# Row maxima interleaved with scores in the attention phases of a two-layer kernel

## The chip, the core and the metric

The kernel runs on one core of a Trainium2 chip. The metric is the device time of one execution in microseconds. Every kernel is timed several times and the median is given; the profile is of one execution more, with its own time.

## What is computed

Two layers on x of 2 x 1024 rows of 128: attention with 16 heads of 64, an expert layer with one expert chosen for each row, a state-space layer, and a dense layer over 8 experts. Only attention is touched:

```python
Q = jnp.einsum('btd,hkd->bthk', x, W_Q) + b_Q
K = jnp.einsum('btd,hkd->bthk', x, W_K) + b_K
V = jnp.einsum('btd,hkd->bthk', x, W_V) + b_V
scores = jnp.einsum('bqhk,bshk->bhqs', Q, K) / jnp.sqrt(jnp.asarray(d_head, x.dtype))
attn = jax.nn.softmax(scores, axis=-1)
out_h = jnp.einsum('bhqs,bshk->bqhk', attn, V)
return jnp.einsum('bqhk,hdk->bqd', out_h, W_O) + b_O
```

## The kernel before

Heads go in pairs, so the two batches have 16 pairs (0 to 15). The two heads of a pair stand on the two halves of the array: for scores and row maxima on the two row halves (64*128 in the profile), for projection, value products, values and sums on the two column halves (128*64). The rows of a sequence are cut into two chunks c of 512 columns, its keys into eight tiles j of 128.

A pair has four phases f. In phase f the kernel makes four scores ("score", for chunk f // 2 and four of the key tiles), and four value products ("pv") of the same tiles. A score (pe_score, L563 and L567) is a matmul of high and low parts, three products and one that subtracts the row's maximum (guard), each on both row halves, eight matmuls in all. ScalarE takes its exponential (L1065) into one of seven prob buffers; the value product (pe_pv, L594) reads that buffer, and GpSimd adds it to the sums (L2013).

The maxima that are subtracted are those of a later pair's rows, and are made while this pair is worked on: "max" (pe_max, L580) is one matmul on each row half with the high parts alone, "maxed" is the reduction by VectorE (dve_max, L1494). When all 16 of a pair are there, "cols" (L1504), "row" and "rowed" turn them into a row, which a DMA spreads into guard. Phase 3 makes maxima for the pair after the next. "proj" (L610) is the projection of a coming pair's keys or queries, followed by a high part by ScalarE (L1039) and a low part by VectorE ("lo", L1487). "values" (L625) and "valued" (L1523, VectorE) make the values of the next pair in phase 1. "out" (L672) is the output product of the pair before, which VectorE adds into x in eight instructions (L1555), in phases 2 and 3; "sum" (L645) makes the divisors from the sums, in phase 0. "take" is ScalarE's copy of the finished value products (L1074). Some phases also have steps of the next stages, from the table EARLY.

One list of steps, built by phase() for pairs 0 to 14 and by last_phase() for pair 15, sets the order on every engine: each engine walks through the list and issues the steps that are its own, in that order. So the order of "score" and "max" in the list is the order in TensorE's queue, and that of "maxed", "lo", "valued" and "out" the one in VectorE's.

PSUM has three slots of two banks for scores, maxima and output products, one bank for the value products that are being summed, and one work bank for projection, values, row and sum. The slots are given in turn, in the order of the list (Banks.plan): each score, maximum or output product waits until the reader of the one three places earlier is done (slots.free): the exponential of a score, the reduction of a maximum, VectorE's group of an output product.

Of the kernel before, what the change touches and what calls it, by code (L numbers as in the profile page):

```python
# [183 lines left out]
def project(pair, chunk):  # L184
    return [("proj", pair, *chunk), ("lo", pair, *chunk)]


def largest(*maxes):

    return [step for m in maxes for step in (("max", *m), ("maxed", *m))]  # L190


def phase(pair, f):


    if pair == LAST:
        return last_phase(f)
    c, js = f // 2, range(NT // 2 * (f % 2), NT // 2 * (f % 2 + 1))
    last, nxt = pair - 1, pair + 1
    if pair == 0:  # L200
        maxes = [(nxt, *m) for m in MAXES[max(6 * f - 2, 0):6 * f + 4]] if f < 3 else [(nxt + 1, *m) for m in MAXES[:4]]
    else:
        maxes = [(nxt, *MAXES[4 * f + 4 + i]) if f < 3 else (nxt + 1, *MAXES[i]) for i in range(4)]
    maxes = [m for m in maxes if m[0] < PAIRS]
    ahead = pair + 2 if f < 3 else pair + 3
    chunks = [(ahead, CHUNKS[(f + 1) % 4])] if ahead < PAIRS else []
    projected = project(*chunks[0]) if chunks else []
    products, found = [("max", *m) for m in maxes], [("maxed", *m) for m in maxes]
    pv = [("pv", pair, c, j) for j in js]
    early = EARLY.get((pair, f), [])  # L210
    order = [("score", pair, c, j) for j in js] + largest(*maxes[:1]) + projected[:1] + pv[:1]
    order += products[1:4] + projected[1:] + found[1:3]
    if f == 1:
        order += [pv[1], ("values", nxt, 0), ("valued", nxt, 0)] + found[3:4]
    else:
        order += found[3:4] + [pv[1]]
    order += largest(*maxes[4:])
    if f == 2:
        order.append(("cols", nxt))
    if f >= 2 and last >= 0:  # L220
        order.append(("out", last, f - 2))
    order.append(pv[2])
    if f == 0:
        order += [("sum", last)] * (last >= 0) + [pv[3]] + early
    elif f == 1:
        order += [pv[3], ("values", nxt, 1), ("valued", nxt, 1)] + early + [("take", pair, c)]
    elif f == 2:
        order += early + [pv[3], ("row", nxt), ("rowed", nxt)]
    else:
        order += early + [pv[3], ("take", pair, c)]  # L230
    return order


def last_phase(f):

    pair, c, js = LAST, f // 2, range(NT // 2 * (f % 2), NT // 2 * (f % 2 + 1))
    order = [("score", pair, c, j) for j in js]
    if f == 1:
        order += [("out", pair - 1, 0), ("out", pair - 1, 1)]
    second = ([("sumhalf", pair, 0)] if f == 3 else []) + EARLY.get((pair, f), [])  # L240
    pv = [("pv", pair, c, j) for j in js]
    order += pv[:2] + second + pv[2:3] + [("sum", pair - 1)] * (f == 0) + pv[3:]
    if f % 2:
        order.append(("take", pair, c))
    if f == 3:
        order.append(("out", pair, 0))
    return order
# [6 lines left out]
def attention_order():  # L254

    order = [("gsum",), ("lnvar", 0), ("lnroot", 0), ("gscale",), ("lnrows", 0), *turned(0), ("bias", 0)]
    keys, queries, more_keys, more_queries = (("proj", 0, *ch) for ch in CHUNKS)
    maxes = [(0, *m) for m in MAXES]
    order += [keys, queries, *largest(*maxes[:2]), more_keys, more_queries, *largest(*maxes[2:4])]
    order += [("full", 0, *ch) for ch in CHUNKS] + largest(maxes[4]) + ahead_of_scores(1, CHUNKS[0]) + largest(*maxes[5:7])  # L260
    order += ahead_of_scores(1, CHUNKS[1]) + largest(*maxes[7:9]) + [("values", 0, 0)] + largest(*maxes[9:11])
    order += ahead_of_scores(1, CHUNKS[2]) + largest(*maxes[11:13]) + ahead_of_scores(1, CHUNKS[3]) + largest(maxes[13])
    order += [("values", 0, 1)] + largest(maxes[14]) + ahead_of_scores(2, CHUNKS[0]) + largest(maxes[15])
    order += [("gdir",), ("cols", 0), ("row", 0), ("valued", 0, 0), ("rowed", 0), ("valued", 0, 1)]
    for pair in range(PAIRS):
        for f in range(4):
            order += phase(pair, f)
    return order
# [2253 lines left out]
```

## Time and profile before

| what | value |
|---|---|
| median of 3 runs | 1196.02 us (1195.93 to 1198.23) |
| span of the profiled execution | 1192.9 us |
| TensorE busy | 1129.3 us, 95% |
| VectorE busy | 816.6 us, 68% |
| GpSimd busy | 759.8 us, 64% |
| ScalarE busy | 600.7 us, 50% |

Attention takes the first 740 us or so of the span. Busy time of an engine is the time in which at least one of its instructions runs; matmuls are pipelined, so the time from the start of one to the start of the next says more than the length shown. In the timeline, instructions of one kind that follow each other are merged into one line with their count; what stands in brackets is the idle time before it and who ended that. PE is TensorE's matmuls, PEld its weight loads, DVE VectorE, ACT ScalarE, POOL GpSimd.

### The profile page before, as it was taken

How to read it: one execution, taken by the hardware profiler on the slowest of the kernel's cores; microseconds unless marked ns; L12 is line 12 of the kernel's file. 1: busy time of each engine (PE TensorE's matmuls, PEld its weight loads, DVE VectorE, ACT ScalarE, POOL GpSimd, SP SyncE). 2: the span in 40 equal slices, each digit the busy share in tenths (PEclk: the TensorE clock that was granted, in tenths of full speed). 3: DMA queues.
4: the chain of work that ended last, by engine and by line, in shares of the span. 5: the costliest groups of instructions: out<-in, count | busy, mean ns of one | idle time of the engine just before them, and what ended most of it. 6: DMA issues, size and time to landing. Idle time of an engine off the chain costs nothing.

```text
span 1192.9 us, 19525 instructions
## 1 busy us (share of the span) xinstructions
PE 1129.3 (95%) x7549; PEld 660.4 (55%) x7549; DVE 816.6 (68%) x1208; ACT 600.7 (50%) x867; POOL 759.8 (64%) x393
## 2 busy tenths in 40 slices
PE   5899999999999999999999999988888998989998
PEld 1445555555555555555555555776644444445786
DVE  5575666655755656655666754723798999998887
ACT  3434345344343444444444344544886664956753
POOL 3477778777777768767678973023089887896100
PEclk9899999999999999999999999998999999999999
DMA  6000000000000000000000204357464544341000
GB/s 199 1 1 2 1 1 1 2 1 1 2 1 2 1 2 1 2 2 1 1 1 11 68 30 147 111 148 223 147 219 135 167 142 158 127 159 54 10 9 18
DMA packets 38076, 68.85 MB, mean 58 GB/s; under 512 B 5952, under 2 KB 24128, under 8 KB 37984
## 3 DMA queue, kind: packets, MB, share of 16 engines
q1 hardware_dynamic: 34976, 64.52, 17.1%
q0 software_dynamic: 1024, 2.10, 0.5%
q8 instruction: 60, 0.98, 0.3%
q10 hardware_dynamic: 1984, 0.98, 0.3%
q14 instruction: 32, 0.26, 0.1%
HBM read 61.30 MB, written 6.16 MB: 57 GB/s over the span
## 4 chain that ended last, share of the span: by engine, by line
PE 78%; issue 7%; DVE 6%; POOL 5%; ACT 2%; DMA 2%; SPq 0%; POOLq 0%; DVEq 0%; ACTq 0%
PE psum L594 20%; PE psum L563 16%; PE psum L580 6%; PE psum L610 6%; PE psum L567 5%; PE psum L974 3%; PE psum L672 3%; PE psum L880 3%; PE psum L957 3%; POOL hc L2101 3%; PE psum L625 2%; PE psum L645 2%; PE psum L749 2%; PE psum L738 1%; DVE psum L1781 1%
## 5 line engine op out<-in xcount | busy, mean ns | idle before, releaser
L2013 POOL TENSOR_TENSOR psums<-psums,prob 128x1024 f32<-128x1024 f32 x180 | 426.9, 2372 | 106.4 <-ACT prob L1065 84.3
L1494 DVE TENSOR_REDUCE mx<-psum 128x2 f32<-128x1024 f32 x256 | 301.8, 1218 | 214.2 <-PE psum L580 214.2
L1065 ACT ACTIVATE prob<-psum 128x1024 f32<-128x1024 f32 x256 | 243.4, 1025 | 218.2 <-PE psum L567 218.2
L594 PE MATMUL psum<-prob,V 128*64 128x512 f32 x1024 | 258.4, 604 | 0.0
L2101 POOL TENSOR_TENSOR hc<-hs,cc 128x1024 f32<-128x1024 f32 x64 | 151.5, 2368 | 21.5 <-DVE hs L1788 19.0
L1788 DVE TENSOR_TENSOR_SCAN hs<-dA,psum 128x1024 f32<-128x1024 f32 x64 | 146.3, 2287 | 2.2
L880 PE MATMUL psum<-hc,ident 128*128 128x512 f32 x256 | 123.6, 606 | 2.5 <-DVE slot_rows_h L1796 1.4
L594 PEld LDWEIGHTS psum<-prob,V 128*64 128x64 f32 x1024 | 62.0, 136 | 98.3 <-issue 92.6
L2013 POOL TENSOR_TENSOR psums<-prob 128x1024 f32<-128x1024 f32 x30 | 71.4, 2382 | 63.4 <-ACT prob L1065 63.4
L563 PE MATMUL psum<-q_hi,k_hi 64*128 64x512 f32 x512 | 108.4, 419 | 0.0
L567 PE MATMUL psum<-guard,row_one 64*128 64x512 f32 x512 | 101.6, 393 | 2.2 <-DMA guard<-mrow 2.2
L563 PE MATMUL psum<-q_hi,k_lo 64*128 64x512 f32 x512 | 101.7, 393 | 0.0
L563 PE MATMUL psum<-q_lo,k_hi 64*128 64x512 f32 x512 | 101.6, 393 | 0.0
L580 PE MATMUL psum<-k_hi,q_hi 64*128 64x512 f32 x512 | 90.2, 425 | 4.0 <-DVE mx L1494 2.3
L1074 ACT COPY oraw<-psum 128x512 f32<-128x512 f32 x32 | 18.8, 587 | 131.8 <-PE psum L594 131.8
L580 PEld LDWEIGHTS psum<-k_hi,q_hi 64*128 64x128 f32 x512 | 43.8, 186 | 67.5 <-issue 48.9
L1555 DVE SCALAR_TENSOR_TENSOR x<-psum,inv,x 128x128 f32<-128x128 f32 x256 | 71.9, 343 | 12.1 <-issue 10.7
L880 PEld LDWEIGHTS psum<-hc,ident 128*128 128x128 f32 x256 | 48.8, 194 | 44.7 <-issue 32.4
L563 PEld LDWEIGHTS psum<-q_hi,k_hi 64*128 64x128 f32 x512 | 48.5, 186 | 38.2 <-issue 17.3
L864 PE MATMUL psum<-xdr,pickr 128*128 128x512 f32 x128 | 57.7, 533 | 10.8 <-DVE hs L1788 10.6
L1287 ACT ACTIVATE dA<-slotT,alog 128x1024 f32<-128x1024 f32 x32 | 36.6, 1150 | 40.0 <-DVE hs L1788 39.7
L567 PEld LDWEIGHTS psum<-guard,row_one 64*128 64x128 f32 x512 | 48.8, 186 | 13.7 <-DMA guard<-mrow 2.6
(290 smaller groups left out, 1686.9 us busy)
## 6 DMA issues: line engine op xcount, KB each, us to landing
cc<-C_rows SPq DMA_DIRECT2D x64, 512.0 KB, 3.7
kq_wts<-in_e_rows SPq DMA_DIRECT2D x14, 578.0 KB, 4.7
e_wts<-in_e_rows SPq DMA_DIRECT2D x10, 578.0 KB, 4.1
e_w<-in_e_rows SPq DMA_DIRECT2D x6, 578.0 KB, 4.3
slots_in<-e_zero SPq DMA_DIRECT2D x2, 960.0 KB, 8.2
slots_out<-e_y SPq DMA_DIRECT2D x30, 64.0 KB, 3.0
x<-in_x SPq DMA_DIRECT2D x2, 512.0 KB, 5.0
e_w<-in_e_w SPq DMA_DIRECT2D x1, 1024.0 KB, 7.8
```

The lines of the kernel that those rows point to most:

```text
L563: pe.matmul(both[:, s, :], left[HALF[s], js], right[HALF[s], cs], start=(part == 0), stop=False)
L567: ins = pe.matmul(both[:, s, :], A.row_one[HALF[s], :], A.guard[q][HALF[s], cs], start=False, stop=True)
L580: ins = pe.matmul(both[:, s, :], A.q_hi[r][HALF[s], t * P:(t + 1) * P], A.k_hi[r][HALF[s], c * CH:(c + 1) * CH], start=True, stop=True)
L594: ins = pe.matmul(A.O[HALF[s], :], A.V[pair % 2][:, j, s * DH:(s + 1) * DH], A.prob[unit(pair, c, j) % NPB][:, s * CH:(s + 1) * CH], start ...
L610: ins = pe.matmul(bank[HALF[s], :], w[:, (2 * p + s) * DH:(2 * p + s + 1) * DH], K.xnT[:, b, c * CH:(c + 1) * CH], start=True, stop=True)
L880: ins = pe.matmul(X.Y[:, c * CH:(c + 1) * CH], K.ident[:, :], X.hc[u % 3][:, c * CH:(c + 1) * CH], start=(u > 0 and n == 0), stop=(n == NS ...
L1065: act.activation(A.prob[n % NPB][:, :], slots.bank("score", pair, c, j).rearrange("p s n -> p (s n)"), ACT.Exp, scale=float(DH) ** -0.5).t ...
L1494: dve.tensor_reduce(K.A.mx[:, :, t, c], slots.bank("max", pair, t, c), AXX, ALU.max).then_inc(*slots.inc("max", pair, t, c))
L1555: ins = dve.scalar_tensor_tensor(out=K.x[:, tile, :], in0=slots.bank("out", pair, c)[:, s, t * P:(t + 1) * P], scalar=A.inv[:, s * NT + 4 ...
L1788: dve.tensor_tensor_scan(X.hs[u % 3][:, :], X.dA[u % 3][:, :], X.gain[u % 2], 0.0, ALU.mult, ALU.add).then_inc(X.state_done, 1)
L2013: pool.tensor_tensor(total[:, :], (K.A.prob[(n - 1) % NPB] if j == 1 else total)[:, :], K.A.prob[n % NPB][:, :], ALU.add).then_inc(*K.psum ...
L2101: pool.tensor_tensor(X.hc[u % 3][:, :], X.hs[u % 3][:, :], X.cc[u % NCC][:, :], ALU.mult).then_inc(X.product_done, 1)
```

## The change

The change is in phase() alone. Before, a phase's list was: four scores, the first maximum with its reduction, the projection, the first value product, three maxima, the low part of the projection and the reductions, the second value product. Now each of the first four maxima, with its reduction, stands ahead of one of the four scores; then come the projection with its low part and the first two value products. In phase 1 the first half of the values follows these, without the reduction that stood behind it. Further maxima (pair 0 has up to six in a phase), cols, out and all after these stay where they are.

```diff
@@ -208,12 +208,13 @@
     products, found = [("max", *m) for m in maxes], [("maxed", *m) for m in maxes]
     pv = [("pv", pair, c, j) for j in js]
     early = EARLY.get((pair, f), [])
-    order = [("score", pair, c, j) for j in js] + largest(*maxes[:1]) + projected[:1] + pv[:1]
-    order += products[1:4] + projected[1:] + found[1:3]
+    scores = [("score", pair, c, j) for j in js]
+    order = []
+    for i, score in enumerate(scores):
+        order += largest(*maxes[i:i + 1]) + [score]
+    order += projected + pv[:2]
     if f == 1:
-        order += [pv[1], ("values", nxt, 0), ("valued", nxt, 0)] + found[3:4]
-    else:
-        order += found[3:4] + [pv[1]]
+        order += [("values", nxt, 0), ("valued", nxt, 0)]
     order += largest(*maxes[4:])
     if f == 2:
         order.append(("cols", nxt))
```

largest() gives for each maximum the steps "max" and "maxed".

## Rows read from the trace of the kernel before

**Rows 1.** The page: busy time and share of the span of each engine.

```profile
PE 1129.3 (95%) x7549; PEld 660.4 (55%) x7549; DVE 816.6 (68%) x1208; ACT 600.7 (50%) x867; POOL 759.8 (64%) x393
```

**Rows 2.** Busy time by stretch: start:end, length, then each engine, TensorE's clock last.

```profile
44.00:49.50 5.50, 5.50 (x26) 4.32 (x28) 0.00 (x0) 3.07 (x3) 1.94 (x1) 0.50 0.00 0
...
200.00:740.00 540.00, 539.26 (x4439) 303.61 (x4436) 327.86 (x518) 233.22 (x279) 398.25 (x176) 1.00 0.04 13
```

**Rows 3.** Timeline of TensorE over phase 1 of a pair: start, length, engine, line.

```profile
509.96 0.50 PE L563 MATMUL psum<-q_hi,k_hi 64*128 64x512 f32 x2
...
513.54 0.39 PE L567 MATMUL psum<-guard,row_one 64*128 64x512 f32 x2
513.77 0.40 PE L580 MATMUL psum<-k_hi,q_hi 64*128 64x512 f32 x2
514.09 1.08 PE L610 MATMUL psum<-xnT,wk 128*64 128x512 f32 x4
515.00 1.03 PE L594 MATMUL psum<-prob,V 128*64 128x512 f32 x4
...
516.85 1.08 PE L594 MATMUL psum<-prob,V 128*64 128x512 f32 x4
...
518.64 1.89 PE L594 MATMUL psum<-prob,V 128*64 128x512 f32 x8
520.35 1.04 PE L625 MATMUL psum<-wv,xnT 128*64 128x128 f32 x16
521.33 0.50 PE L563 MATMUL psum<-q_hi,k_hi 64*128 64x512 f32 x2
```

**Rows 4.** The same phase, timeline of the other engines.

```profile
511.20 3.80 ACT L1065 ACTIVATE prob<-psum 128x1024 f32<-128x1024 f32 x4 [6.78 <-PE psum L567]
...
514.21 1.23 DVE L1494 TENSOR_REDUCE mx<-psum 128x2 f32<-128x1024 f32 x1 [4.79 <-PE psum L580]
515.22 0.69 ACT L1039 ACTIVATE k_hi<-psum,bk 128x512 fp32r<-128x512 f32 x1 [0.23 <-PE psum L610]
...
515.94 0.75 DVE L1487 SCALAR_TENSOR_TENSOR k_lo<-psum,bk,k_hi 128x512 fp32r<-128x512 f32 x1 [0.51 <-ACT k_hi L1039]
...
516.61 2.35 DVE L1494 TENSOR_REDUCE mx<-psum 128x2 f32<-128x1024 f32 x2
...
521.44 0.69 DVE L1523 TENSOR_TENSOR V<-psum,bv 128x512 f32<-128x512 f32 x1 [0.76 <-PE psum L625]
```

**Rows 5.** Timeline before the first phase: maxima that wait for VectorE.

```profile
30.34 2.35 DVE L1494 TENSOR_REDUCE mx<-psum 128x2 f32<-128x1024 f32 x2
...
31.61 0.19 PEld L580 LDWEIGHTS psum<-k_hi,q_hi 64*128 64x128 f32 x2 [0.53 <-DVE mx L1494]
...
32.04 0.65 PE L610 MATMUL psum<-xnT,wk 128*64 128x512 f32 x2
...
36.85 0.50 PE L580 MATMUL psum<-k_hi,q_hi 64*128 64x512 f32 x2
...
37.40 1.23 DVE L1494 TENSOR_REDUCE mx<-psum 128x2 f32<-128x1024 f32 x1 [0.19 <-PE psum L580]
```

**Rows 6.** Timeline at the starts of two phases with VectorE work of the later stage.

```profile
191.87 0.50 PE L563 MATMUL psum<-q_hi,k_hi 64*128 64x512 f32 x2
192.86 0.64 DVE L1449 BATCH_NORM_AGGREGATE mv<-stats 128x2 f32<-128x6 f32 x8
...
618.01 0.50 PE L563 MATMUL psum<-q_hi,k_hi 64*128 64x512 f32 x2
619.94 0.17 DVE L1642 CAST e_owneri<-e_owner 128x15 int32<-128x15 f32 x1
```

**Rows 7.** Timeline: an output product and the VectorE group that reads it.

```profile
739.66 1.95 PE L672 MATMUL psum<-wo,oraw 64*128 64x128 f32 x32
740.82 4.49 DVE L1555 SCALAR_TENSOR_TENSOR x<-psum,inv,x 128x128 f32<-128x128 f32 x16 [4.42 <-issue]
```

**Rows 8.** Timeline before the first phase: the longest wait of TensorE there.

```profile
43.91 0.80 PE L567 MATMUL psum<-guard,row_one 64*128 64x512 f32 x2 [2.20 <-DMA guard<-mrow]
```

## The prediction

> **What bounds the kernel now.** I read the page first. TensorE is busy for 95% of the span, VectorE for 68%, no other engine for more [rows 1]. The busy time by stretch says it more sharply: from 200 to 740 us TensorE is busy for 539.26 of 540.00 us at clock 1.00, VectorE for 327.86, ScalarE for 233.22 and GpSimd for 398.25 [rows 2]. So in attention the order of TensorE's own queue is the time, and every other engine follows it. That leaves two ways to change the time: TensorE's work gets shorter or longer by itself, or a wait appears in a queue that now has none. The change does both, so I took one phase apart.
>
> **What a phase costs.** Phase 1 of a pair runs from 509.96 to 521.33 [rows 3]. A score is four pairs of matmuls on the two row halves of the array; pairs follow each other by 0.23 us (513.54 to 513.77), so a score takes 0.93 and a row maximum 0.23. Value products work on the two column halves, 0.86 each (518.64 to 520.35 is two of them). Projection to value product is 0.91. The first pair of rows after column work takes 0.10 more. Start to the projection: 514.09 - 509.96 = 4.13, which is 0.10 + 4 x 0.93 + 0.23 and 0.09 for the change to columns. From the first value product to the second are 516.85 - 515.00 = 1.85, though the product takes 0.86 and the three maxima 0.69: going to rows and back to columns costs 0.30.
>
> **Part one: a round trip goes.** Today a phase goes to rows twice before its value products are under way (scores and first maximum, then three maxima); after the change once. The trip's 0.30 is saved in every phase that has maxima: 59 (pairs 0 to 14 have 60 phases, and the last of them has no maxima left; pair 15 has an order of its own, untouched). Saved: 59 x 0.30 = 17.7 us. The out products on rows in phases 2 and 3 keep their own trip.
>
> The Trainium skill, page "TensorEngine Tiling (Array Packing)", section "Key Properties", says that changing the tiling mode drains TensorE. The trace agrees, with the 0.30 above; by this rule alone the change would be a gain of 17.7 us.
>
> **Part two: a wait comes.** Scores and maxima share three PSUM slots in turn, so each instruction waits for the reader of the slot three places earlier. Today S0 S1 S2 S3 M0 come in a row, and the readers of S0 and S1 (exponentials) have two scores' time; M0's reader (the VectorE reduction) has the projection, a value product and two maxima. After the change the queue is M0 S0 M1 S1 M2 S2 M3 S3, and S1 takes M0's slot. Between them lie S0 and M1 only.
>
> How long is a maximum's slot held? The reduction starts 0.44 after its matmuls (513.77 to 514.21), 0.55 where these pay the change to rows (36.85 to 37.40), and takes 1.22 to 1.23 [rows 3 to 5]. The release is seen where maxima already wait for VectorE, ahead of the first phase: the reduction begun at 30.34 ends at 31.56, and TensorE starts at 31.61, 0.05 later; it then needs 0.43 to the next work (32.04) where an unhindered maximum needs 0.32 (513.77 to 514.09), because its weights were not loaded beside earlier work: 0.10 more [rows 3, 5].
>
> Now the run, with time 0 at M0. S0 at 0.33, M1 at 1.26, and S1 could start at 1.49. M0's slot is released at 0.55 + 1.22 + 0.05 = 1.82, and S1 counts as started at 1.92: 0.43 late. M2 is then at 2.85. M1's reduction starts when VectorE is free, at 1.70, its slot is loaded for S2 at 3.07, and S2 could start at 3.08: no wait. M2's reduction starts at 3.29, so S3 counts as started at 3.29 + 1.22 + 0.05 + 0.10 = 4.66 and ends at 5.59. M3 waits for S1's exponential: an exponential starts 1.24 after its score's first pair when the load is not hidden (509.96 to 511.20) and takes 1.01 (four with three steps of 0.93 between them take 3.80) [rows 4], so M3 is at about 4.2, which is still ahead of S3's limit. Without any wait the run would end at 0.10 + 4 x 1.16 = 4.74. The waits cost 0.85 a phase, and the change to columns comes as before.
>
> Before, these parts took 4.13 + (1.85 - 0.86) = 5.12; after 5.59 + 0.09 = 5.68. Net +0.56 (0.85 of waits less the 0.30 of part one). 59 x 0.56 = 33.0 us. Queued behind each wait on TensorE is everything, as it runs in order: the next maximum, the projection and all value products.
>
> **Part three: what VectorE does when a phase starts.** Today the first reduction comes 4.3 us into the phase, and whatever VectorE still has from the phase before is covered (its idle time ahead of 514.21 is 4.79) [rows 4]. After the change M0's reduction is due at 0.55, and each microsecond that VectorE is busy beyond that moves S1 and all behind it.
> Values: after phase 1 the second value addition runs from 521.44 to 522.13, phase 2 having begun at 521.33. With the next instruction issued some 0.07 before its end the reduction starts at 0.74, 0.19 late, in 15 phases: 2.9 us [rows 3, 4].
> Output groups: VectorE starts 1.16 after an out product and takes 4.49/2 = 2.25 for one; the next phase starts about 2.9 after the product (half of 1.95 and a trip of 0.2, and two value products). It ends at 0.5: nothing [rows 7].
> Later stages' steps: the statistics end 1.63 after their phase began (191.87, 193.50), which costs 1.1, twice; the owner list ends 2.10 after (618.01, 620.11), of which the value addition has 0.19: 1.4; four smaller ones of the same kind I put at 1.6 together, an estimate from these two. 5.2 us [rows 6].
> Projection: it keeps the single work bank until VectorE has written the low part. Now the high part waits for the fourth exponential (at about 6.8) and takes 0.69, the low part 0.75: 8.3. The first values product in phase 1 is due at 5.68 + 0.91 + 2 x 0.86 = 8.3 and needs the bank and its weights at 8.4: 0.14 in 14 phases, 2.0 us. In the other phases the bank's next user comes later: nothing.
> GpSimd adds the probabilities and is busy for 398 of 540 us [rows 2]; the phase gets longer, its work does not: nothing. The row and its DMA stay where they were behind the value products, a whole phase or more ahead of their reader: nothing. DMA queues are not moved past.
>
> **Sum.** 33.0 + 2.9 + 5.2 + 2.0 = 43.1 us. The profiled execution has a span of 1192.9, the median is 1196.0, so 3.1 lie outside; 1196.0 + 43 = 1239.
>
> Bounds: each wait has its nearest row, but no row shows a score that waits for a reduction. At the low end the weights' load is hidden after a wait and the maximum counts 0.44: S1 and S3 are 0.10 each, S1 another 0.11 earlier, 0.31 a phase or 18 us less, and part three's later stages come to nothing: 1239 - 18 - 5 = 1216. At the high end M3's wait adds to S3's and every reduction is late by what its issue costs behind another (1.23 instead of 1.13 apart), 0.25 a phase: 1254. I take the middle, as 0.10 and 0.55 are rows of the same matmul.
>
> **Rivals.**
> (a) Faster: slots come back in time and only the trip is gone, 1196.0 - 17.7 = 1178. It decides at 1.39 us from a maximum to the score two places on; the rows give 0.44 + 1.22 + 0.05 = 1.71. For it speaks that the two scores in a row of today never wait, and that a wait's attribution in a trace is inferred. Against it, the waits that maxima have ahead of phase 0.
> (b) Small waits: only S1 waits, or S3's wait falls under M3's, so that waits are 0.43 to 0.5 a phase: net 0.13 to 0.2, which is 8 to 12 us, and with 2 to 10 of part three 1206 to 1218; at the point where waits are 0.30, no change, 1196.
> (c) VectorE as the bound: all three of S1, S2 and S3 wait as long as S1 (3 x 0.43), and leftovers of VectorE push on from phase to phase by 0.1: 1.4 a phase instead of 0.85, 59 x 0.55 = 32 more, 1271. Against: VectorE works 327.86 of 540 us.
> (d) The clock falls. After the wait of 2.20 us that ends at 43.91, TensorE ran from 44.0 to 49.5 at clock 0.50 (1.2 GHz), and a stretch like this costs half its 5.5 us [rows 2, 8]. The new waits are 0.3 us each, and short waits of 0.2 to 0.5 before phase 0 left the clock high. Were there one such stretch in each of 15 pairs, 41 us more: 1280.
> The Trainium skill, page "TensorE: Matmul & The Clock Gate", section "A second HAM failure mode: psum-queue depth-cycling", describes a kernel whose small idle gaps between groups, from cycling through PSUM banks, make the clock oscillate; that is (d).
>
> **How the numbers follow.** Forecast 0.68; (a) 0.11; (b) 0.15, of which 0.03 within 0.2%; (c) 0.04; (d) 0.02. The forecast's own range is 1216 to 1254; taking in (b) but for its no-change end, the range is 1206 to 1254, and (a), (c), (d) and that end, 0.20 together, are left out. A measurement of this kernel can tell about 0.2% from no change. Faster 0.11, same 0.03, slower 0.68 + 0.12 + 0.04 + 0.02 = 0.86.
>
> **What would show it.** In the profile after: TensorE's busy share in attention falls below 95%, with idle time ahead of L563's weight loads released by the reduction L1494, about 0.3 to 0.4 ahead of S1 and 0.1 to 0.2 ahead of S3, none ahead of S2; phases of 11.9 to 12.1 us where they were 11.4; four reductions close together from 0.55 after a phase's start; the projection directly followed by two value products at 0.86 each; clock 1.00. The prediction is wrong if a score can start without the reduction's release, if the reduction starts much sooner than 0.44 after its matmuls, or if the change to rows costs more than 0.30 elsewhere.

## The result and the profile after

The changed kernel takes 1231.24 us (median of 4 runs, 1229.62 to 1232.13), the kernel before 1195.97 beside it; the ratio is 1.0286 with a 95% interval of [1.0274, 1.0298]. It is 35 us slower, where the prediction had 43 (1239, range 1206 to 1254).

The page after: the same number of instructions, TensorE at 93%, and a first row of slices that still looks full. The stretch from 200 to 740 us, which answers to [rows 2], shows a loss: 526.71 us busy where it was 539.26, with the clock at 1.00 as before. It shows only about half of it: a matmul is drawn 0.40 us long where the next follows 0.23 behind it, so the first 0.17 of a wait lies under the matmul before. (In the changed kernel all lines below the edit have a number one higher: L564 is a score, L581 a maximum, L595 a value product, L1495 the reduction.)

```profile
span 1229.6 us, 19525 instructions
...
PE 1146.0 (93%) x7549; PEld 653.3 (53%) x7549; DVE 829.3 (67%) x1208; ACT 617.6 (50%) x867; POOL 759.9 (62%) x393
...
PE   5899999999999999999999999996979999889998
...
PEclk9899999999999999999999999998999999999999
```

```profile
200.00:740.00 540.00, 526.71 (x4187) 282.44 (x4185) 325.33 (x494) 236.11 (x269) 385.02 (x171) 1.00 0.02 7
```

The waits from 60 to 780 us (engine, line, waited for: us in total, times, longest):

```profile
PEld psum L564 <- DVE mx L1495: 61.5, 147, 2.1
...
PEld psum L581 <- ACT prob L1066: 22.4, 57, 0.4
...
PE psum L564 <- DVE mx L1495: 17.1, 57, 1.7
```

In the trace before, the reduction L1494 held TensorE up in attention almost nowhere. Now 147 weight loads of scores (L564) wait for it, 61.5 us in all and 2.1 us at most, and 57 of maxima (L581) wait for exponentials. These sums are idle time of the weight loads, much of it beside matmuls that still run; what a wait costs is read from the starts of the steps below. M0 to M3 are the maxima of a phase, S0 to S3 its scores.

This is phase 1 of the pair whose phase stands in [rows 3] and [rows 4]: start, length, engine, line.

```profile
530.73 0.50 PE L581 MATMUL psum<-k_hi,q_hi 64*128 64x512 f32 x2
...
531.06 0.39 PE L564 MATMUL psum<-q_hi,k_hi 64*128 64x512 f32 x2
...
531.27 2.39 DVE L1495 TENSOR_REDUCE mx<-psum 128x2 f32<-128x1024 f32 x2 [1.08 <-PE psum L581]
...
532.55 0.19 PEld L564 LDWEIGHTS psum<-q_hi,k_hi 64*128 64x128 f32 x2 [0.60 <-DVE mx L1495]
532.55 0.51 PE L564 MATMUL psum<-q_hi,k_hi 64*128 64x512 f32 x2 [0.16 <-DVE mx L1495]
...
533.59 0.40 PE L581 MATMUL psum<-k_hi,q_hi 64*128 64x512 f32 x2
...
533.83 0.39 PE L564 MATMUL psum<-q_hi,k_hi 64*128 64x512 f32 x2
...
534.87 0.19 PEld L581 LDWEIGHTS psum<-k_hi,q_hi 64*128 64x128 f32 x2 [0.39 <-ACT prob L1066]
...
535.32 0.18 PEld L564 LDWEIGHTS psum<-q_hi,k_hi 64*128 64x128 f32 x2 [0.26 <-DVE mx L1495]
...
536.44 1.08 PE L611 MATMUL psum<-xnT,wk 128*64 128x512 f32 x4
...
537.35 1.89 PE L595 MATMUL psum<-prob,V 128*64 128x512 f32 x8
...
539.10 1.09 PE L626 MATMUL psum<-wv,xnT 128*64 128x128 f32 x16
...
542.71 0.50 PE L581 MATMUL psum<-k_hi,q_hi 64*128 64x512 f32 x2
```

Times from the phase's start at 530.73, beside the run that the prediction worked out: S1 loads at 1.82 (1.82), S2 starts at 3.10 (3.08, no real wait), M3 at 4.14 (4.2), S3 at 4.59 (4.56), the projection at 5.71 (5.68). The bracket of S1's weight load names the reduction. After the projection two value products and the values follow in one run, 1.75 us from the first product to the values: 0.86 each and 0.03.

The whole of attention, by the starts of its phases in the two traces (us, mean of the pairs without work of a later stage):

| phase | before | after | more | predicted |
|---|---|---|---|---|
| 0 | 11.50 | 12.00 | 0.50 | 0.56 |
| 1 | 11.37 | 11.96 | 0.59 | 0.70 |
| 2 | 11.23 | 11.80 | 0.57 | 0.75 |
| 3 | 10.98 | 11.37 | 0.39 | 0.56 |

From the first phase's start to the last pair's are 685.1 us before and 718.9 after, 33.8 more. The rest of the program has 3.1 more in this pair of profiles, but it ranged from 465.3 to 472.3 us over all twelve profiles of this study, whose kernels are alike there; that part is not the change's.

### The profile page after: what moved, and what is told of

Its sections match the earlier page's. It is cut to its first block, busy times and chain, and to the rows that moved or that the text cites. A ratio compares the mean times of both kernels' runs of the same rounds, so it can differ in the third digit from the quotient of the medians.

```text
span 1229.6 us, 19525 instructions
## 1 busy us (share of the span) xinstructions
PE 1146.0 (93%) x7549; PEld 653.3 (53%) x7549; DVE 829.3 (67%) x1208; ACT 617.6 (50%) x867; POOL 759.9 (62%) x393
## 4 chain that ended last, share of the span: by engine, by line
PE 67%; DVE 17%; issue 8%; POOL 4%; ACT 2%; DMA 1%; another core or an unknown queue 0%; SPq 0%; POOLq 0%; ACTq 0%; DVEq 0%
PE psum L595 15%; PE psum L564 14%; DVE mx L1495 6%; PE psum L611 5%; PE psum L581 4%; PE psum L568 4%; DVE x L1556 4%; PE psum L975 3%; PE psum L881 3%; PE psum L958 3%; POOL hc L2102 2%; PE psum L626 2%; PE psum L646 2%; PE psum L673 2%; PE psum L750 1%
## 5 line engine op out<-in xcount | busy, mean ns | idle before, releaser
L1066 ACT ACTIVATE prob<-psum 128x1024 f32<-128x1024 f32 x256 | 261.1, 1026 | 283.8 <-PE psum L568 275.5
L1495 DVE TENSOR_REDUCE mx<-psum 128x2 f32<-128x1024 f32 x256 | 307.8, 1224 | 60.9 <-PE psum L581 59.5
L595 PE MATMUL psum<-prob,V 128*64 128x512 f32 x1024 | 245.4, 598 | 0.0
L564 PE MATMUL psum<-q_hi,k_hi 64*128 64x512 f32 x512 | 114.4, 443 | 17.3 <-DVE mx L1495 17.3
L595 PEld LDWEIGHTS psum<-prob,V 128*64 128x64 f32 x1024 | 67.3, 137 | 110.9 <-issue 90.0
L581 PE MATMUL psum<-k_hi,q_hi 64*128 64x512 f32 x512 | 115.8, 451 | 3.3 <-DVE mx L1495 1.6
L564 PE MATMUL psum<-q_lo,k_hi 64*128 64x512 f32 x512 | 101.3, 392 | 0.0
L564 PE MATMUL psum<-q_hi,k_lo 64*128 64x512 f32 x512 | 101.3, 392 | 0.0
L564 PEld LDWEIGHTS psum<-q_hi,k_hi 64*128 64x128 f32 x512 | 48.3, 185 | 70.3 <-DVE mx L1495 62.5
L581 PEld LDWEIGHTS psum<-k_hi,q_hi 64*128 64x128 f32 x512 | 48.3, 186 | 67.5 <-issue 28.4
```

Of the source, the lines that this page charges most:

```text
L564: pe.matmul(both[:, s, :], left[HALF[s], js], right[HALF[s], cs], start=(part == 0), stop=False)
L581: ins = pe.matmul(both[:, s, :], A.q_hi[r][HALF[s], t * P:(t + 1) * P], A.k_hi[r][HALF[s], c * CH:(c + 1) * CH], start=True, stop=True)
L595: ins = pe.matmul(A.O[HALF[s], :], A.V[pair % 2][:, j, s * DH:(s + 1) * DH], A.prob[unit(pair, c, j) % NPB][:, s * CH:(s + 1) * CH], start ...
L1066: act.activation(A.prob[n % NPB][:, :], slots.bank("score", pair, c, j).rearrange("p s n -> p (s n)"), ACT.Exp, scale=float(DH) ** -0.5).t ...
L1495: dve.tensor_reduce(K.A.mx[:, :, t, c], slots.bank("max", pair, t, c), AXX, ALU.max).then_inc(*slots.inc("max", pair, t, c))
```

## The experiments

The theory: (T) a phase now contains two slot times of a maximum in series (M0's ahead of S1, M2's ahead of S3), 0.85 us, and saves one trip to rows. Rivals to it, in capitals to tell them from those of the prediction: (A) maxima and scores in turn are dear on TensorE by themselves; (B) VectorE's load is the bound. Each ratio is to runs of the kernel before on the same chip.

### A shorter reader, in the changed kernel and in the kernel before

```diff
-    dve.tensor_reduce(K.A.mx[:, :, t, c], slots.bank("max", pair, t, c), AXX, ALU.max).then_inc(*slots.inc("max", pair, t, c))
+    dve.tensor_reduce(K.A.mx[:, :, t, c], slots.bank("max", pair, t, c)[:, :, 0:CH // 2], AXX, ALU.max).then_inc(*slots.inc("max", pair, t, c))
```

> The changed kernel, but each reduction of a maximum reads only the first 256 of the 512 columns of each head: it leaves out half of the keys in the row maxima. Theory (a score waits for the slot of the maximum three places earlier, and the gain is the saved trip to rows): a reduction falls from 1.22 us to about 0.7, so M0's slot is back at about 1.3 us where S1 could start at 1.49; no score waits for a reduction. Maxima then wait for exponentials (M2 for S0, 0.2 us a phase). A phase is shorter than the kernel before's by 0.15 in phases 0 to 2 and up to 0.3 in phase 3: about 1184 us (1180 to 1190), that is 47 below the changed kernel. Rival A (alternating maxima and scores is dear by itself, on TensorE): stays within 10 us of 1231. Rival B (VectorE's load is the bound): it falls too, but so should the same edit of the kernel before.

> The kernel before with the same shorter reduction (half of the keys left out of the row maxima), the control of the run above. Theory: nothing on TensorE waits for reductions there but the output product in phases 2 and 3, which seems to wait 0.16 us for the second maximum's reduction (1.12 us from value product to output product, where the changed kernel has 0.96): 28 x 0.16 = 4.5 us less, about 1191 (1189 to 1194). Rival B (VectorE's load): it falls by tens of us as well.

Measured: the changed kernel with it 0.9932 [0.991, 0.9955], the kernel before with it 0.9945 [0.9928, 0.9961]. Times 1195.97 that is 1188 and 1189. The same edit takes 42 us (1.0286 less 0.9932) from the changed kernel and 7 from the kernel before. VectorE's load from 200 to 740 us fell alike in both (325.33 to 247.23 us, and 327.86 to 240.49), and only the changed kernel gained tens of us, so the load by itself, (B), is not the bound; the order on TensorE is unchanged, so (A) is out. Phase 1 of the same pair, timeline:

```profile
502.27 0.69 DVE L1495 TENSOR_REDUCE mx<-psum 128x2 f32<-128x512 f32 x1 [1.08 <-PE psum L581]
...
502.99 0.41 PE L581 MATMUL psum<-k_hi,q_hi 64*128 64x512 f32 x2
...
503.23 0.41 PE L564 MATMUL psum<-q_hi,k_hi 64*128 64x512 f32 x2
...
504.28 0.18 PEld L581 LDWEIGHTS psum<-k_hi,q_hi 64*128 64x128 f32 x2 [0.38 <-ACT prob L1066]
...
506.81 0.20 PEld L611 LDWEIGHTS psum<-xnT,wk 128*64 128x64 f32 x4 [0.37 <-issue]
```

The reduction takes 0.69, S1's first pair starts at 503.23, 1.50 after the phase began, with no wait. What is left are two waits of maxima for exponentials, 0.25 together (the run ends at 5.08, unhindered it would be 4.83), which is why a phase gains 0.05 to 0.25 and not 0.35. The expected 1184, in whose range of 1180 to 1190 the result lies, left out that five phases with work of a later stage still lose 0.5 to 1.2 each, 4 us in sum. In the control, phases 2 and 3 are shorter by 0.11: that is the wait of the output product. Phase 2 of pair 0 is shorter by 2.2 in both; its row stands behind six reductions.

### The order within the run

```diff
     for i, score in enumerate(scores):
-        order += largest(*maxes[i:i + 1]) + [score]
+        order += largest(*maxes[:1]) * (i == 0) + [score] + largest(*maxes[i:i + 1]) * (i > 0)
```

> The changed kernel with the run M0 S0 S1 M1 S2 M2 S3 M3: one trip to rows as in the change, but M0 and M1 have two scores behind them. Theory: S1 no longer waits; S2 waits 0.2 for S0's exponential, S3 0.2 for M1's reduction; the run ends at 5.16 us instead of 5.59: 59 x 0.43 = 25 us less than the changed kernel, about 1206 (1200 to 1212), still above the kernel before. Rival A (mixing them in one run costs by itself): near 1231.

Measured: 1.0052 [1.0035, 1.0068], 1202 us: 28 us less than the changed kernel by the ratios, with all reads whole and still one trip.

```profile
512.45 0.50 PE L581 MATMUL psum<-k_hi,q_hi 64*128 64x512 f32 x2
...
513.73 0.40 PE L564 MATMUL psum<-q_hi,k_hi 64*128 64x512 f32 x2
...
515.01 0.19 PEld L564 LDWEIGHTS psum<-q_hi,k_hi 64*128 64x128 f32 x2 [0.40 <-ACT prob L1066]
...
516.36 0.19 PEld L564 LDWEIGHTS psum<-q_hi,k_hi 64*128 64x128 f32 x2 [0.24 <-DVE mx L1495]
...
517.75 1.08 PE L611 MATMUL psum<-xnT,wk 128*64 128x512 f32 x4
```

Against the kernel before it is still 6 us slower. S1 (513.73) waits for nothing; the waits are those expected, S2 for an exponential and S3 for a reduction, and the run ends at 5.30 with the change to columns (expected 5.25). In plain phases it is 0.1 to 0.2 slower than before in phases 0 and 1, and even in 2 and 3. (A) is out a second time: the same instructions in one run, 28 us apart by the order of the slots alone.

### A longer reader

```diff
+    dve.tensor_reduce(K.A.extra[:, :, t, c], slots.bank("max", pair, t, c)[:, :, 0:P // 2], AXX, ALU.max)
     dve.tensor_reduce(K.A.mx[:, :, t, c], slots.bank("max", pair, t, c), AXX, ALU.max).then_inc(*slots.inc("max", pair, t, c))
...
+            A.extra = sba("extra", [P, 2, NT, NC])
```

> The changed kernel with one small reduction (64 columns of each head, into a tile of its own) ahead of each reduction of a maximum: it adds work and takes nothing away. It holds each maximum's slot about 0.2 us longer. Theory: the run's length contains two slot times of a maximum in series (M0's ahead of S1, M2's ahead of S3), so a phase grows by 2 x 0.2 = 0.4 us and the kernel by 59 x 0.4 = 24 us: 1255 (1247 to 1265). Rival B (VectorE's rate of four reductions a phase): 4 x 0.2 x 59 = 47 us more, 1278. Rival A: no change from 1231.

Measured: 1.0507 [1.0477, 1.0538], 1257 us, 26 above the changed kernel by the ratios.

```profile
549.53 0.19 PEld L581 LDWEIGHTS psum<-k_hi,q_hi 64*128 64x128 f32 x2 [0.81 <-issue]
...
550.07 0.29 DVE L1495 TENSOR_REDUCE extra<-psum 128x2 f32<-128x128 f32 x1 [1.08 <-PE psum L581]
...
550.28 1.22 DVE L1496 TENSOR_REDUCE mx<-psum 128x2 f32<-128x1024 f32 x1
...
551.55 0.19 PEld L564 LDWEIGHTS psum<-q_hi,k_hi 64*128 64x128 f32 x2 [0.79 <-DVE mx L1496]
...
552.88 0.19 PEld L564 LDWEIGHTS psum<-q_hi,k_hi 64*128 64x128 f32 x2 [0.34 <-DVE mx L1496]
...
554.49 0.19 PEld L564 LDWEIGHTS psum<-q_hi,k_hi 64*128 64x128 f32 x2 [0.45 <-DVE mx L1496]
...
555.63 1.08 PE L611 MATMUL psum<-xnT,wk 128*64 128x512 f32 x4
```

The small reduction puts the large one back by 0.21 (550.07 to 550.28). S1 loads 2.02 after the start instead of 1.82, the projection comes at 6.10 instead of 5.71: two slot times, not four. The phase grew by 0.4. That is (T)'s number and half of (B)'s.

### One maximum ahead of the scores

```diff
-    order = [("score", pair, c, j) for j in js] + largest(*maxes[:1]) + projected[:1] + pv[:1]
+    order = largest(*maxes[:1]) + [("score", pair, c, j) for j in js] + projected[:1] + pv[:1]
```

> The kernel before with one step moved: the first maximum and its reduction stand ahead of the four scores, the other three maxima stay behind the first value product, so the two trips to rows stay. Theory (what costs in the change is the slot order, not that a maximum stands ahead of a score): M0 has two scores behind it before its slot is needed, no wait in a plain phase; where VectorE still has work of a later stage at the phase's start (five phases) S2 waits up to 1 us: 0 to 4 us more than the kernel before, ratio 1.000 to 1.003. Rival A (a maximum at the head of a phase is dear by itself): more than 10 us.

Measured: 1.0154 [1.0128, 1.0181], 18 us more: the expectation was wrong, and the number alone would speak for (A), which had more than 10. The phases decide. Plain phases 1 and 2 are unchanged to 0.02, so a maximum at the head is not dear by itself; plain phases 3 and the phases 0 after them lose 0.6 and 0.45, and phases with work of a later stage up to 1.5. The timeline across the start of a phase 3, at 356.37:

```profile
355.41 2.29 DVE L1555 SCALAR_TENSOR_TENSOR x<-psum,inv,x 128x128 f32<-128x128 f32 x8
...
356.37 0.50 PE L580 MATMUL psum<-k_hi,q_hi 64*128 64x512 f32 x2
...
357.75 0.19 PEld L563 LDWEIGHTS psum<-q_hi,k_hi 64*128 64x128 f32 x2 [0.40 <-DVE x L1555]
...
357.81 1.22 DVE L1494 TENSOR_REDUCE mx<-psum 128x2 f32<-128x1024 f32 x1
...
359.07 0.19 PEld L563 LDWEIGHTS psum<-q_hi,k_hi 64*128 64x128 f32 x2 [0.57 <-DVE mx L1494]
```

In this kernel the three late reductions still stand ahead of the output product's eight VectorE instructions, which therefore begin at 355.41, one microsecond ahead of the next phase, and not 1.16 after the product. S1 now takes the output product's slot and waits for them (0.40), and M0's reduction starts only at 357.81, so S2 waits as well (0.57). The prediction had costed this leftover at nothing for the changed kernel, rightly, because there the reductions are all done by then. A maximum ahead of the scores pays when VectorE is clear, and not otherwise.

### Output products inside the run of scores

If slots and trips are the price, the output products of phases 2 and 3, which have a trip of their own, should pay when they stand where every slot has its reader's time.

Phase 3 alone:

```diff
-    order = [("score", pair, c, j) for j in js] + largest(*maxes[:1]) + projected[:1] + pv[:1]
+    scores = [("score", pair, c, j) for j in js]
+    within = f == 3 and last >= 0
+    if within:
+        order = largest(*maxes[:1]) + scores[:3] + [("out", last, 1)] + scores[3:] + projected[:1] + pv[:1]
+    else:
+        order = scores + largest(*maxes[:1]) + projected[:1] + pv[:1]
...
-    if f >= 2 and last >= 0:
+    if f == 2 and last >= 0:
```

> The kernel before with phase 3 of pairs 1 to 14 as M0 S0 S1 S2 out S3, projection, P0, three maxima, P1, P2, P3: the output product, which has a trip to rows of its own today, goes into the run of scores, at a place where each slot has its reader's time. Theory: a trip of 0.35 and a wait of 0.11 less in 14 phases, 5 to 6 us less than the kernel before, ratio 0.9955. Rival (VectorE's group of 2.3 us behind the output product holds back the reductions and with them TensorE): no gain or a loss.

Measured: 1.0006 [0.9995, 1.0017], nothing where 5 to 6 us less were expected; this is the rival's outcome. The plain phases 3 are 0.15 to 0.2 longer, for the reason just seen: phase 2's output product keeps VectorE busy across the border, S1 and S2 wait. In pairs 3, 9 and 10, whose phase 2 is longer and lets VectorE finish, phase 3 is 0.41 to 0.50 shorter, and in pair 14, which has no maxima left, 0.39; in pairs 12 and 13 it is 1.08 and 0.61 longer.

Phase 2 alone:

```diff
+    if f == 2 and last >= 0 and projected:
+        order = largest(*maxes[:1]) + scores[:1] + products[1:2] + projected[:1] + products[2:3] + scores[1:2] + found[1:3]
+        order += scores[2:3] + [("out", last, 0)] + scores[3:] + products[3:4] + pv[:1] + found[3:4] + [("cols", nxt)]
+        return order + pv[1:3] + projected[1:] + early + [pv[3], ("row", nxt), ("rowed", nxt)]
```

> The kernel before with phase 2 of pairs 1 to 13 as M0 S0 M1, projection, M2 S1 S2 out S3 M3, then the four value products: two trips to rows instead of three, each slot with its reader's time between. Theory: 13 x 0.4 = 5 us less than the kernel before, ratio 0.9955. Rival as in the run above: no gain or a loss, the row at the phase's end waiting for the late reduction of M3.

Measured: 0.9978 [0.9964, 0.9991], 2.6 us less where 5 were expected. Plain phases 2 take 10.78 instead of 11.23. (Here L585 is a maximum, L615 the projection, L677 the output product, L599 a value product.)

```profile
515.63 0.50 PE L585 MATMUL psum<-k_hi,q_hi 64*128 64x512 f32 x2
...
517.22 1.08 PE L615 MATMUL psum<-xnT,wq 128*64 128x512 f32 x4
...
518.23 0.50 PE L585 MATMUL psum<-k_hi,q_hi 64*128 64x512 f32 x2
...
520.41 1.05 PE L677 MATMUL psum<-wo,oraw 64*128 64x128 f32 x16
...
522.23 0.40 PE L585 MATMUL psum<-k_hi,q_hi 64*128 64x512 f32 x2
...
522.55 0.20 PEld L599 LDWEIGHTS psum<-prob,V 128*64 128x64 f32 x4 [0.37 <-issue]
```

From 518.23 to 522.55 the run M2 S1 S2 out S3 M3 has no wait. The gain of 0.46 in plain phases is a trip of 0.35 and the output product's wait of 0.11. The phases 2 of pairs 3, 9, 10 and 12, and phase 3 of pair 13, lost 0.25 to 0.65 instead; they have steps of the next stage.

Both, with the order of the second experiment in phases 0 and 2 of pair 0:

```diff
+    if pair == 0 and f in (0, 2):
+        order = largest(*maxes[:1]) + scores[:2] + largest(*maxes[1:2]) + scores[2:3] + largest(*maxes[2:3]) + scores[3:]
+        order += largest(*maxes[3:4]) + projected + pv[:2] + largest(*maxes[4:]) + [("cols", nxt)] * (f == 2) + pv[2:3]
+        return order + (pv[3:] + early if f == 0 else early + [pv[3], ("row", nxt), ("rowed", nxt)])
```

> Both moves of the output product together, and phases 0 and 2 of pair 0 in the order M0 S0 S1 M1 S2 M2 S3 M3 with one trip (these two phases were shorter by 0.7 and 1.4 us with that order). Theory: 5.6 + 5.2 + 2.1 = 13 us less than the kernel before, ratio 0.989 (0.987 to 0.993); a version below both kernels.

Measured: 0.9948 [0.9927, 0.9968], 6 us less instead of 13. Now that phase 2 leaves VectorE clear, plain phases 3 have 10.49 to 10.53 instead of 10.99, as expected of them. The rest went in crowded phases: +0.69 and +1.23 in phases 2 and 3 of pair 12, +0.82 in phase 3 of pair 13, 0.3 each in phase 2 of pairs 3, 9 and 10. Pair 0's two phases gave 0.6 and 1.0 of the 2.1 expected of them.

Without the moves there:

```diff
-    if f == 2 and last >= 0 and projected:
+    if f == 2 and last >= 0 and projected and pair not in (3, 9, 12):
...
-    within = f == 3 and last >= 0
+    within = f == 3 and last >= 0 and pair not in (12, 13)
...
-    if f == 2 and last >= 0:
+    if f >= 2 and last >= 0 and not within:
```

> The version with both moves of the output product, without them in the phases where they lost time: phase 2 of pairs 3, 9 and 12 (+0.30, +0.28, +0.69 us) and phase 3 of pairs 12 and 13 (+1.23, +0.82), where steps of the next stage crowd VectorE. Theory (phases add up, and a phase's loss comes from its own readers): 3.3 us less than that version, 11 us less than the kernel before, ratio 0.991 (0.989 to 0.994). Rival (the moves shift waits from phase to phase, so taking some back loses the neighbours' gain): 0.995.

Measured: 0.9913 [0.9897, 0.9929], 1185.6 us by the ratio, 10 below the kernel before and 45 below the changed one, and faster than both; 11 below the kernel before were expected. Pair 12's phases and phase 2 of pairs 3 and 9 are back to their old length; phase 2 of pair 10, which kept the move, still has its 0.25. Phase 3 of pair 13 is not back (+0.68). It lost as much (+0.65) in the kernel with phase 2 alone moved, so that loss comes from the move in the phase ahead of it: the rival has this one case.

### The trip by itself

```diff
-    order += products[1:4] + projected[1:] + found[1:3]
-    if f == 1:
-        order += [pv[1], ("values", nxt, 0), ("valued", nxt, 0)] + found[3:4]
+    if f < 2:
+        order += products[1:3] + projected[1:] + found[1:3] + pv[1:2] + products[3:4]
+        order += [("values", nxt, 0), ("valued", nxt, 0)] * (f == 1) + found[3:4]
+    else:
+        order += products[1:4] + projected[1:] + found[1:3]
+    if f < 2:
+        pass
     else:
         order += found[3:4] + [pv[1]]
```

> The kernel before with one more trip to rows and no other change of what waits: in phases 0 and 1 of pairs 0 to 14 the third of the three maxima stands behind the second value product. It measures the trip by itself, 30 times. By the phases compared so far a trip costs 0.35 us (0.10 into rows, 0.20 out of them for the first weight load and 0.05 on the next product): 10.5 us more, ratio 1.0088. By the prediction's 0.30: 9 us, 1.0075. Rival (the 0.35 are waits of maxima for exponentials, not the change of tiling): less than 3 us, as the third maximum then has more time.

Measured: 1.0104 [1.0083, 1.0125], 12 us for 30 trips. By phases: 26 of the 30 are longer by 0.31 to 0.38, with a mean of 0.35, while phases 2 and 3 are unchanged to 0.03. (Here L584 is a maximum, L598 a value product, L629 the values.)

```profile
522.93 0.73 PE L584 MATMUL psum<-k_hi,q_hi 64*128 64x512 f32 x4
...
523.59 0.20 PEld L598 LDWEIGHTS psum<-prob,V 128*64 128x64 f32 x4 [0.36 <-issue]
...
524.60 0.19 PEld L584 LDWEIGHTS psum<-k_hi,q_hi 64*128 64x128 f32 x2 [0.81 <-issue]
...
525.03 1.09 PE L629 MATMUL psum<-wv,xnT 128*64 128x128 f32 x16
```

From 523.59 to 525.03 are 1.44 us for a value product (0.86) and a maximum (0.23): 0.35 for going back to rows and leaving them once more. No engine is named as waited for in these lines. Of the other four phases two are of pair 0, and two of pair 3 are 1.15 longer; in those the clock fell, as the last section has it.

## Why the prediction was right, point by point

- What bounds the kernel: right. TensorE's queue was full and every change in it moved the time one to one; phases add up, and the extra time of the 60 phases (33.8 us) is the median's 35.3 within what the rest of the program varies.
- Part two, the run with its waits, was right to 0.03 us at each step but M3, which waits 0.06 less than said and costs nothing. It came from rows of the kernel before alone: 0.44 or 0.55 until the reduction starts, 1.22 for it, 0.05 for the release, 0.10 for a weight load that is not hidden. The longer reader confirmed that two slot times are in series; the shorter reader and the other order took the cost away.
- Part one, the trip, was mis-sized: 0.30 predicted, 0.35 measured by itself. The part missed is 0.05 on the first value product after rows (517.76 - 516.85 = 0.91 in [rows 3], against 0.86), 59 x 0.05 = 3.0 us.
- "A wait in a queue that now has none" was not quite so: in phases 2 and 3 the output product already waited for a reduction, 0.11 by the control with the shorter reader. The change does away with it, 28 x 0.11 = 3.1 us. The trace before gave no releaser for it; it showed only as idle time of 0.89 ahead of the output product's weight load, as in the line below, where other changes to rows have 0.81.

```profile
529.31 1.00 PEld L672 LDWEIGHTS psum<-wo,oraw 64*128 64x128 f32 x16 [0.89 <-issue]
```

- Part three, VectorE's leftovers: the value addition cost phase 2 what was said (S1 at 2.00 instead of 1.82). The later stages' steps were put at 5.2; the phases concerned (1 of pairs 3 and 9, 1 to 3 of pair 12, 0 of pair 13) have 5.3 above their like. Output groups: nothing, right. The low part's wait was put at 0.14 a phase and was 0.03: 1.5 us.
- Pair 0 was taken as any other, 2.6 us more, and is 0.4 shorter: its first maximum now fills time in which scores wait for the first guard (2.20 us before, 1.96 after), and in phase 2 its row no longer waits so long for late reductions. 3.0 us. The size is not firm. Both kernels had the clock at 0.50 for 6.8 us in pair 0's phase 0; the kernel with phase 2 alone moved, whose phase 0 there has the order of the kernel before, had 3.4 us of it in its profile, and that phase was 1.3 us shorter.
- These four, 3.0 + 3.1 + 1.5 + 3.0 = 10.6, make the difference of 9.3 between 43.1 and 33.8, but for 1.3.
- Of the signs that were to show it, one failed: TensorE's busy share from 200 to 740 us is 97.5%, not below 95%. A phase is 0.4 to 0.6 longer, but the 0.17 of each wait that lies under the matmul before it does not show as idle time.
- The rivals: (a) fell with the first trace, as S1 waits. (b) fell with the same trace: the projection came at 5.71, so that the waits are 0.88 a phase and not 0.43 to 0.5. Waits of the size that (b) had, some 0.45, came with the order M0 S0 S1 M1 S2 M2 S3 M3, which was measured at 1202. (c) fell there too, as S2 starts with no wait to speak of, and with the longer reader, which added two slot times and not four. (d): the clock was 1.00 from 200 to 740 us in the changed kernel; its waits, some 0.4 us and one of 1.7, did not bring it down. The Trainium skill's account of a clock that oscillates with small gaps ("TensorE: Matmul & The Clock Gate", section "A second HAM failure mode: psum-queue depth-cycling") is not what this kernel shows from 200 to 740 us. With a longer reader the clock fell once, as the last section has it.

## What to carry to other kernels

With slots given in turn, write down for each user the time from its first matmul to its reader's release, and place behind it at least that much of other work before the slot comes round; here the first maximum has 1.49 us until S1 could start, where 1.82 are needed, and needs two scores behind it. A trip between row and column tiling costs 0.35 us, less than the waits that its removal brought; where both can be had (an output product among scores, 0.46 a phase), look first at what the reader's engine still has to do when the phase starts. A step of another stage that today lies under scores has its cover only as long as nobody waits for that engine at once.

## What the runs showed of the hardware that was not expected

The releaser column had no name for waits that end while an engine changes tiling: the idle time reads as "issue" with 0.81 us, and a wait of 0.1 on top of it shows only as 0.89. Comparing the start-to-start times of the same pair of steps in two orders (1.12 and 0.96 from value product to output product: 0.05 of it is the first value product after rows, the rest the wait) found it.

TensorE's clock fell in the middle of attention in two of the twelve profiles. With the longer reader, in phase 2 of pair 12, whose start is crowded on VectorE, a score waited 1.84 us, and some 1.7 us later the clock was at its lower level (1.2 GHz) for 3.4 us: pairs of matmuls 0.43 apart instead of 0.23.

```profile
670.27 0.50 PE L564 MATMUL psum<-q_hi,k_hi 64*128 64x512 f32 x2 [1.84 <-DVE mx L1496]
...
672.35 0.63 PE L564 MATMUL psum<-q_hi,k_lo 64*128 64x512 f32 x2
672.77 0.63 PE L568 MATMUL psum<-guard,row_one 64*128 64x512 f32 x2
```

This is rival (d), once in a kernel, at a cost of about 1.1 us: the phase is 1.5 longer than in the changed kernel, where the longer reader makes others 0.4 longer. The longest idle time of the same kind in the changed kernel, 1.7 us, left the clock at 1.00, so that it was the wait that brought the clock down is not shown.

In the kernel with an extra trip the same happened without a wait; the columns are as in [rows 2].

```profile
176.00:200.00 24.00, 23.96 (x202) 12.77 (x198) 14.98 (x36) 9.65 (x12) 18.21 (x12) 0.93 0.00 1
```

TensorE was busy for 23.96 of 24.00 us around it. The clock was at 0.50 for 3.4 us from 191.5, just behind a sums step of 64 matmuls of one column each, and phases 0 and 1 of pair 3 each have 0.8 us more than the others from it. The same step stands in the phases 0 of all the kernels, and the clock did not fall behind it elsewhere in attention; what brought it down here stays open.
